# Delta-rule attention with a quantized FFN on one core: the first span rebuilt, with rounding constants made by ScalarE

## What is computed

```python
def l2n(x):
    return x / jnp.maximum(jnp.sqrt(jnp.sum(x * x, axis=-1, keepdims=True)), 1e-12)

def _quantized_matmul(x, w, scale):
    wq = w.astype(jnp.float8_e4m3fn).astype(x.dtype)
    y = jnp.einsum('bsi,io->bso', x, wq)
    return y * scale

def step(S, inp):                       # delta rule, over the 4096 tokens
    qt, kt, vt, bt = inp
    v_pred = jnp.einsum('bhk,bhkv->bhv', kt, S)
    delta = (vt - v_pred) * bt[..., None]
    S = S + kt[..., None] * delta[:, :, None, :]
    return (S, jnp.einsum('bhk,bhkv->bhv', qt, S))

xn = _layernorm(x, axis=-1)
q, k, v = l2n(heads(xn @ Wq)) * dh ** -0.5, l2n(heads(xn @ Wk)), heads(silu(xn @ Wv))
beta = jax.nn.sigmoid(xn @ Wb)
o = delta_rule(q, k, v, beta)           # scan of step
o = o * jax.lax.rsqrt(jnp.mean(o * o, axis=-1, keepdims=True) + EPS) * o_norm_weight
attn = o.reshape(b, l, d) @ Wo
gate = silu(_quantized_matmul(xn, gate_w, gate_scale))      # 512 x 1536
up = _quantized_matmul(xn, up_w, up_scale)                  # 512 x 1536
ffn = _quantized_matmul(gate * up, down_w, down_scale)      # 1536 x 512
return x + attn + ffn
```

## Time and profile before

| | us |
|---|---|
| median of 3 runs | 2445.73 |
| lowest and highest run | 2445.45, 2448.61 |
| the profiled execution, its own time | 2442.38 |
| its span, first to last instruction | 2440.6 |

### The profile page before, as it was taken

How to read it: one execution, slowest core, us unless ns; L and a number is a source line. 1 busy time by engine, 2 the same in 40 slices (tenths; PEclk the granted TensorE clock), 3 DMA queues, 4 the chain that set the end, 5 groups by cost and what they waited for, 6 DMA issues and landing times.

```text
span 2440.6 us, 90080 instructions
## 1 busy us (share of the span) xinstructions
PE 2314.6 (95%) x40944; PEld 1259.3 (52%) x40944; DVE 1817.7 (74%) x3210; ACT 861.2 (35%) x2069; POOL 275.0 (11%) x521
## 2 busy tenths in 40 slices
PE   1869999999999999999999999999999999999996
PEld 0435555554655545455554555555465554545553
DVE  7985866869677695867769586686967769586785
ACT  2353432524234252423425243242423425242341
POOL 3011002010010101001010110201001010100100
PEclk9989999999999999999999999999999999999999
DMA  6100100100010010100001010010101001010000
GB/s 216 48 1 4 36 3 3 36 3 36 4 36 3 3 36 3 36 3 12 27 3 36 3 36 3 3 36 3 36 4 36 3 3 36 3 36 3 11 28 19
DMA packets 27163, 54.30 MB, mean 22 GB/s; under 512 B 5152, under 2 KB 5152, under 8 KB 26784
## 3 DMA queue, kind: packets, MB, share of 16 engines
q1 hardware_dynamic: 26784, 48.55, 5.7%
HBM read 31.76 MB, written 16.78 MB: 20 GB/s over the span
## 4 chain that ended last, share of the span: by engine, by line
PE 93%; DVE 4%; issue 1%; SPq 1%; DMA 0%; POOL 0%; ACT 0%; POOLq 0%; DVEq 0%
PE T L350 22%; PE D L425 21%; PE D L502 15%; PE D L435 14%; PE D L436 13%; PE D L366 7%; PE D L355 1%; DMA ds_row<-in_L_ffn_down_scale_dram 0%; DVE wd L267 0%; DVE wgu L267 0%; DVE w_lo L921 0%; DVE outer_v L1145 0%; DVE at L1152 0%; SPq L300 0%; SPq L295 0%
## 5 line engine op out<-in xcount | busy, mean ns | idle before, releaser
L435 PE MATMUL D<-xt_hi,wgu 128*128 128x512 f16 x1536 | 586.3, 382 | 18.5 <-ACT sg L674 12.1
L436 PE MATMUL D<-xt_lo,wgu 128*128 128x512 f16 x1536 | 584.7, 381 | 0.0
L425 PE MATMUL D<-xt_hi,w_hi 128*128 128x512 f16 x832 | 317.1, 381 | 38.5 <-DVE wo_lo L925 38.5
L425 PE MATMUL D<-xt_lo,w_hi 128*128 128x512 f16 x832 | 316.5, 380 | 0.0
L502 PE MATMUL D<-wd,f_hi 128*128 128x512 bf16 x768 | 293.6, 382 | 0.3 <-issue 0.3
L425 PE MATMUL D<-xt_hi,w_lo 128*128 128x512 f16 x768 | 292.3, 381 | 0.0
L502 PE MATMUL D<-wd,f_lo 128*128 128x512 bf16 x768 | 291.1, 379 | 0.0
L1152 DVE TENSOR_TENSOR at<-at,outer_v 128x62 f32<-128x62 f32 (+15 forms) x496 | 262.4, 529 | 12.8
L1145 DVE TENSOR_TENSOR outer_v<-mt,at 128x62 f32<-128x62 f32 (+15 forms) x496 | 260.7, 526 | 11.7
L435 PEld LDWEIGHTS D<-xt_hi,wgu 128*128 128x128 f16 x1536 | 150.5, 98 | 195.7 <-ACT sg L674 12.6
L436 PEld LDWEIGHTS D<-xt_lo,wgu 128*128 128x128 f16 x1536 | 150.9, 98 | 167.4 <-issue 2.8
(11 more groups left out here) (169 smaller groups left out, 3207.4 us busy)
## 6 DMA issues: line engine op xcount, KB each, us to landing
xs<-_attn_hidden_states_dram SPq DMA_DIRECT2D x34, 512.0 KB, 3.4
out_dram<-xs SPq DMA_DIRECT2D x32, 512.0 KB, 3.1
f_hi<-in_L_ffn_down_w_dram SPq DMA_DIRECT2D x2, 768.0 KB, 6.8
f_lo<-in_L_ffn_down_w_dram SPq DMA_DIRECT2D x2, 768.0 KB, 8.3
qt<-in_L_ffn_gate_w_dram SPq DMA_DIRECT2D x2, 768.0 KB, 4.3
kpv<-in_L_ffn_up_w_dram SPq DMA_DIRECT2D x2, 768.0 KB, 4.3
qt<-in_L_attn_Wq_dram SPq DMA_DIRECT2D x1, 1024.0 KB, 10.2
kpv<-in_L_attn_Wk_dram SPq DMA_DIRECT2D x1, 1024.0 KB, 13.1
```

The source lines that it names most:

```text
L425: last = nc.tensor.matmul(D[bank][:, :], w[:, k, cols], xp[:, k, :], start=n == 0, stop=n == len(products) - 1)
L435: nc.tensor.matmul(D[bank][:, :], wgu[:, k, c:c + P], xt_hi[:, k, :], start=k == 0, stop=False)
L436: last = nc.tensor.matmul(D[bank][:, :], wgu[:, k, c:c + P], xt_lo[:, k, :], start=False, stop=k == KT_ - 1)
```

## The change

It touches only the first span and what comes before it.

- **Constants.** ScalarE makes abs(w) * 2^20 as bf16 in one activation (`magnitude_of`), into other places than before. VectorE then computes max(c, 1.5 * 2^14) - w and max(c, 1.5 * 2^14) - that, two SCALAR_TENSOR_TENSORs per piece, in place of four instructions. For the two GpSimd pieces VectorE applies the max (`unit_of`).
- **Loads.** Wk comes before Wq; pieces 2 to 5 get stages of their own and are issued early; Wb and the norm weight are issued by ScalarE; the three scale vectors are issued behind piece 6. The norm weight has its own semaphore, `onw_loaded`.
- **Weights.** The order of largest magnitudes, high and low parts and rounding is changed on VectorE; Wk comes first. TensorE waits at job 0 for the low part of Wk only, at the other jobs for Wq's, at V for all.
- **Norms.** The eight squares have eight buffers, and the 96 one-column products run in one go behind job 8, in bank 3. The root of the bound is taken by GpSimd ahead of the Newton steps for k.
- **VectorE's loop.** In the first span too, V's transposes stand in the solve loop; two down pieces stand at steps 14 and 18; the fuses have a table of their own, starting at step 22. Two memsets are moved to the front.
- **ScalarE.** The 12 scalings of `wd` stand in pairs behind the silus of tiles 4 to 9; in `order` rows below their line is L726.

```diff
-NORM_BANK = 0
+NORM_BANK = 3
+LEAST, STEP_UP = 1.5 * 2.0 ** 14, 2.0 ** 20
+FUSE_FIRST_AT = {22: 0, 26: 1, 30: 2, 34: 3, 38: 4, 43: 5, 48: 6, 53: 7, 59: 8}
+DOWN_PIECE_AT = {14: 2, 18: 3}
...
+            load_w(1, kt, wk)
             load_w(0, qt, wq)
-            load_w(1, kt, wk)
+            load_piece(P_PIECES)
             load_w(2, vt, wv)
-            sp.dma_start(wb_raw[:, :, :], wb.rearrange("(k p) c -> p k c", p=P)).then_inc(w_loaded[3], 16)
-            for h in range(QUADS):
-                sp.dma_start(onw4[32 * h:32 * h + 32, :], onw.rearrange("(d o) -> d o", o=1), allow_slow_non_contiguous=True).then_inc(small_loaded, 16)
             load_w(4, pt, wo)
-            load_piece(P_PIECES)
-            load_piece(P_PIECES + 1)
...
+            for n in range(P_PIECES + 1, P_PIECES + 4):
+                load_piece(n)
             for n in range(P_PIECES):
                 sp.wait_ge(p_rounded, n + 1)
                 load_piece(GU_PIECES + 2 * n)
                 load_piece(GU_PIECES + 2 * n + 1)
...
+            sp.wait_ge(v_rounded, 3)
+            load_piece(P_PIECES + 4)
+            sp.dma_start(gs[:, :], gate_s.rearrange("(c p) -> p c", p=P), allow_slow_non_contiguous=True).then_inc(small_loaded, 16)
...
+            sp.dma_start(ds_row[:, :], down_s.partition_broadcast(P)).then_inc(small_loaded, 16)
+            sp.wait_ge(v_rounded, 4)
+            load_piece(P_PIECES + 5)
...
-            pe.wait_ge(proj_ready, 5)
...
+                        if opening and job in JOB_V and bank_of(job) == NORM_BANK:
...
+                        if opening and not first:
+                            pe.wait_ge(proj_ready, 2 if job == JOB_K[0] else 5 if job in JOB_V else 3)
...
+                    if opening:
+                        pe.wait_ge(kwide_ready, MS)
+                        for n in range(GU_PIECES):
+                            pe.wait_ge(sq_ready, n + 1)
+                            for c in range(IC):
+                                last = nc.tensor.matmul(D[NORM_BANK][:, 12 * n + c:12 * n + c + 1], squares[n][:, c * P:(c + 1) * P], ones[:, :],
+                                                        start=True, stop=True)
+                            last.then_inc(norms_full, 1)
                     gram(4)
                     gram(5)
                     project(9, end=5)
...
+                nc.scalar.activation(magnitude(n), stage[where], ACT.Abs, scale=STEP_UP).then_inc(magnitude_ready, 1)
+            for n in range(P_PIECES):
+                magnitude_of(n)
...
-            act.wait_ge(small_loaded, 16 * 7)
+            magnitude_of(P_PIECES)
+            act.wait_ge(onw_loaded, 16 * QUADS)
...
+            for n in range(P_PIECES + 1, P_PIECES + 4):
...
+            for n, src in ((1, kt), (0, qt), (2, vt)):
...
+            magnitude_of(P_PIECES + 4)
+            def square_of(n):
+                if n < P_PIECES:
+                    act.wait_ge(p_rounded, n + 1)
+                    act.wait_ge(proj_ready, 3)
+                else:
+                    act.wait_ge(v_rounded, (n if n < 6 else 7) - P_PIECES + 1)
+                    act.wait_ge(proj_ready, 4 if n in (4, 5) else 3)
+                nc.scalar.activation(squares[n], rounded_home(n), ACT.Square).then_inc(sq_ready, 1)
...
+                    if opening:
+                        magnitude_of(GU_PIECES - 1)
...
+                    if opening:
+                        square_of(0)
+                        square_of(1)
+                        magnitude_of(GU_PIECES)
+                        magnitude_of(GU_PIECES + 1)
+                        beta_tanh()
+                        square_of(2)
+                        evacuate_k(2)
+                        square_of(3)
+                        square_of(4)
+                        evacuate_q(2)
+                        square_of(5)
+                        evacuate_k(3)
+                        square_of(6)
+                        square_of(7)
+                        evacuate_q(3)
+                        magnitude_of(GU_PIECES + 2)
+                        magnitude_of(GU_PIECES + 3)
+                        act.wait_ge(small_loaded, 48)
...
+                        if opening and ic >= 4:
+                            act.wait_ge(wd_rounded, PIECES - GU_PIECES)
+                            for row in (2 * ic - 8, 2 * ic - 7):
+                                ins = nc.scalar.activation(wd[:, row, :], wd[:, row, :], ACT.Identity, scale=row_inv[:, row:row + 1])
+                            if row == IC - 1:
+                                ins.then_inc(wd_ready, 1)
...
+                    if opening:
+                        pool.wait_ge(bound2_ready, 1)
+                        pool.nop(nofuse=True)
+                        nc.gpsimd.tensor_tensor(b_b[:, :], b_a[:, :], pos_half[:, :], ALU.pow).then_inc(bound_ready, 1)
...
+                w, c = stage[slot(n)[0]], magnitude(n)
+                dve.wait_ge(magnitude_ready, n + 1)
+                one(nc.vector.scalar_tensor_tensor(w, c, LEAST, w, ALU.max, ALU.subtract))
+                nc.vector.scalar_tensor_tensor(rounded_home(n), c, LEAST, w, ALU.max, ALU.subtract).then_inc(done, 1)
...
+            def unit_of(n):
+                dve.wait_ge(magnitude_ready, n + 1)
+                nc.vector.tensor_scalar(magnitude(n), magnitude(n), LEAST, None, ALU.max).then_inc(unit_ready, 1)
...
+            one(nc.vector.memset(state[:, :, :, :], 0.0))
+            nc.vector.memset(ssq[:, :], 1.0).then_inc(ffn_ready, 1)
+            unit_of(0)
             dve.wait_ge(rstd_ready, 1)
             for j in range(TILES):
                 layer_norm_apply(j, 0).then_inc(xn_ready, 1)
+            unit_of(1)
+            largest(1, flat(kt))
...
+            rounded(P_PIECES, v_rounded)
             dve.wait_ge(onw_done, 1)
             largest(4, flat(pt))
-            for n in range(P_PIECES, P_PIECES + 2):
-                rounded(n, v_rounded)
+            rounded(P_PIECES + 1, v_rounded)
+            rounded(P_PIECES + 2, v_rounded)
...
+            one(nc.vector.tensor_scalar(wb_out[:, :, :, 0:MS], wb_in, w_scale[:, 3:4], None, ALU.mult))
...
+            dve.wait_ge(hi_ready, 1)
+            low_w(1, kt)
+            dve.wait_ge(hi_ready, 2)
+            low_w(0, qt)
+            rounded(P_PIECES + 3, v_rounded)
+            dve.wait_ge(hi_ready, 3)
+            low_w(2, vt)
...
-                        for n in range(P_PIECES + 2, GU_PIECES):
-                            rounded(n, v_rounded)
-                            if n == P_PIECES + 3:
-                                b_to_tokens()
-                        dve.wait_ge(v_rounded, GU_PIECES - P_PIECES)
-                        one(nc.vector.memset(state[:, :, :, :], 0.0))
+                        rounded(GU_PIECES - 2, v_rounded)
+                        b_to_tokens()
+                        rounded(GU_PIECES - 1, v_rounded)
                         dve.wait_ge(consts, 3 + QUADS)
-                        nc.vector.memset(ssq[:, :], 1.0).then_inc(ffn_ready, 1)
...
                         for n in range(2):
                             rounded(GU_PIECES + n, wd_rounded)
-                            dve.wait_ge(wd_rounded, n + 1)
-                        for m in range(MS):
-                            v_to_tokens(m)
-                        for n in range(2, 4):
-                            rounded(GU_PIECES + n, wd_rounded)
-                            dve.wait_ge(wd_rounded, n + 1)
                         gate_up_bound()
                         set_diagonal(0)
...
+                    fuse_at = FUSE_FIRST_AT if opening else FUSE_AT
...
-                        if op in V_AT and not opening:
+                        if op in V_AT:
                             v_to_tokens(V_AT[op])
                         if opening and op == SCALE_AT:
                             gate_up_scale()
...
+                        if opening and op in DOWN_PIECE_AT:
+                            rounded(GU_PIECES + DOWN_PIECE_AT[op], wd_rounded)
+                        if op in fuse_at:
+                            fuse_tile(fuse_at[op])

```

152 lines of the change are left out of this document (52 added, 100 removed).

## The result

The changed kernel takes **2417.9 us** (median of 4 runs, 2415.18 to 2421.81) against 2445.59 for the kernel before (4 runs, 2441.31 to 2448.61). The ratio is 0.9892, 95% interval 0.9881 to 0.9904: 27.7 us less, where 29.7 were forecast. The profiled execution took 2418.15 us, with a span of 2416.3.

The account below looks back on a forecast made before the run. VectorE was taken to bound the first 234 us, behind TensorE's waits. The loop's end 28.5 us earlier plus 1.2 for the wd scaling made 29.7, so 2445.7 becomes 2416.0 us; range 2411 to 2424.

Parts of the forecast that it names:

- The price of a piece: VectorE's rounding: two instructions of 1.79 us replace four, saving 1.88 us on each of 10 pieces, 18.8 us.
- rival (b): VectorE's rounding: the mixed bf16/f32 form costs 2.22 us, 8.6 us over 20 instructions, giving 2424.6; chance 0.05.
- The start of the projections: Opening of the first span: job 0 waits only for Wk's low part and starts at 45.5 us instead of 58.25.
- rival (c): Opening: more is won, as POOL's 9.4 us follow the maxima and TensorE's clock holds; 2411 to 2413, chance 0.08.
- the onw wait of 6.7 is gone: Opening: VectorE's 6.7 us wait for the norm weight applied to Wo, traced to a DMA, disappears.
- From there to the solve loop: First span, from first projection to first solve step: the solve loop starts at 88.8 us instead of 122.78.
- rival (a): Before the solve loop: a helper, ScalarE or a load, binds and costs 4 to 8 us; 2420 to 2424, chance 0.14.
- late next: Before the solve loop: norms cost TensorE 3 us, covered by VectorE with 1.8 us to spare; first to slip.
- The loop: First span's solve loop grows from 50.99 to 56.4 us and ends at 145.2 instead of 173.77, 28.5 us earlier.
- Rival (d): Gate-up in the loop: TensorE's clock never rises between short waits, 30.3 us more, 2446.3; chance 0.02.
- The moved fuses cost nothing: Solve loop: VectorE sets the pace, so fuses starting at step 22 add no time.
- The 1.2 us for the scaling of wd: Behind the loop: scalings between silus remove most of a 1.5 us TensorE stand, winning 1.2 us.

Follow-up runs that it names:

- e1: Changed kernel with two more one-input passes over the elements in each of VectorE's ten roundings; 2435.32 us, ratio 0.9951.
- b1: Changed kernel with VectorE's first-span order changed: last maximum and scales earlier, pieces moved, three down pieces before the bound; 2422.35 us, ratio 0.9896.
- e7: Changed kernel with GpSimd's second pair of additions made to wait until VectorE has rounded piece 2; first projection at 49.3 us.
- e2: Changed kernel with the three scale vectors loaded right behind Wo and ScalarE's product of Wo waiting for them; 2420.6 us in one run.
- e4: Changed kernel with the first span's fuses at the steps of the other spans, the first at step 29; 2418.07 us in one run.
- e5: Changed kernel with ScalarE's 12 scalings of wd in one block, as before the change; 2419.57 us in one run.
- e10: Changed kernel with the 96 norm products cut into four blocks of 24, three products of job 9 between each two; 2423.58 us, ratio 0.9902.
- b3: Changed kernel with VectorE's order changed again, norm products in four blocks, and gate products ahead of the wait at the loop's end; 2419.34 us, ratio 0.9877.

## Why the prediction was right, step by step

**The price of a piece** was right: 1.79 forecast, 1.75 and 1.76 measured, for one bf16 and one f32 input, with f32, f16 or bf16 output; rival (b), 2.22, is out. The abs on ScalarE took 1.48 against 1.5. e1 shows that these instructions are indeed on the path that sets the end: given back, 19.9 us of them cost 14.2.

**The start of the projections** came out at 45.16 for 45.5 by luck: two errors cancel. GpSimd's result was forecast for 39.5 and was there at 34.2, earlier even than the 37.1 that rival (c) took, and not for the reason of (c), that the time follows the maxima (b1, below). VectorE was forecast to wait 1.6 us for it from 37.9 and instead was itself busy until 39.06, 2.2 of that for the port that GpSimd held. The forecast had left this collision out: it summed the additions and the pieces each for itself, although its own times let them overlap (additions until 28, piece 2 from 24.8). What sets the all-reduce's start is left open. In the changed kernel it came 6.12 us behind the last addition and just behind the last maximum (32.22). In b1, where the last maximum was there at 28.17, it still came 6.1 behind the addition, at 32.62:

```profile
32.62 0.40 POOL L793 PARTITION_ALL_REDUCE amax_all<-amax  x1 [6.12 <-issue]
```

In e7 it was 7.2 behind it, and in no kernel less than 6.0. A part of that time is therefore GpSimd's own; why it was 9.41 in the earlier trace rows no run here tells.

**The loads.** ScalarE issued wb_raw and onw in 0.48 and 2.20 us, where SP had taken 3.83 and 4.43; the table was loaded by 4.8 and the first abs stood at 9.11, waiting for its data. Timeline of the queues, and ScalarE's product, which waits for Wo alone:

```profile
0.81 0.48 ACTq L568 DMA_DIRECT2D wb_raw<-in_L_attn_Wb_dram  x1
...
1.32 2.20 ACTq L570 DMA_DIRECT2D onw<-_attn_o_norm_weight_dram  x4
```

```profile
23.98 2.00 ACT L592 ACTIVATE kpv<-kpv,onw 128x2048 f32<-128x2048 f32 x1 [1.26 <-DMA kpv<-in_L_attn_Wo_dram]
```

The step "the onw wait of 6.7 is gone" holds; e2 adds that the order alone would have hidden most of it.

**From there to the solve loop** 44.94 for 43.3. The bound was ready at 84.0 (84.9 forecast), K3's evacuation stood at 72.0 (73.1), piece 7's abs ended at 56.5 (58.0): ScalarE was earlier than feared, and rival (a), a helper that binds, did not come. VectorE's wait for K3's evacuation, 1.7 us where 0.9 was forecast, looks like the rival's sign, but ScalarE itself had waited for TensorE there (0.62). The start of TensorE was read wrongly: the forecast says 3.4 us at 1.2 GHz "as before", but before the change 14 products were slow, for 5.9 us. It did no harm, since the jobs' distances were taken from that same trace; that this time varies from 2.9 to 5.9 us in equal code, and moves the solve loop by up to 1.2, was not foreseen. What slipped is what the forecast named as "late next", the norms, but not by their length (2.5 us, forecast 3): behind them the clock fell to half, the grams took 2.62 (123 of 128) and 3.06 where they take 2.0 at full clock, and VectorE, which came to them 0.5 earlier than forecast, waited 1.51 us. In e4 and e5, where the low clock lasted half as long, it waited 0.21 and 0.36. Another 0.6 is the first transpose of V, which stands just ahead of the first solve step and was counted in the loop.

**The loop** took 54.90 for 56.4. That transpose is 0.6 of it, the two pieces took 6.9 instead of 7.2, and the last 0.6 are not accounted for. Of the old wait for the bound nothing is left.

**TensorE in the loop.** It waits for fuse, not for silu, from its restart at 112.29 (forecast 112.6). Rival (d), that the clock never rises in this rhythm, is out. Windows of that stretch (length, TensorE busy, granted clock, DMA share, GB/s):

```profile
112.30:116.00 3.70, 3.70 (x10) 0.56 0.29 113
116.00:120.00 4.00, 4.00 (x20) 1.00 0.02 4
...
132.00:136.00 4.00, 3.20 (x15) 1.00 0.00 0
136.00:140.00 4.00, 3.40 (x16) 1.00 0.00 0
```

Eight products at half clock, then 2.4 GHz for the rest. The gaps came out smaller than forecast at first, probably because the late start had let banks fill; from 128 us on there is one in each 4 us, of 0.36, 0.90 and 0.60, and the clock stays. The Trainium skill's rule (TensorE: Matmul & The Clock Gate, section "A second HAM failure mode: psum-queue depth-cycling"), that short idle times between groups of products can make the clock swing, did not come true at this length of gap; the clock did fall in the 3.88 us without work at the loop's end, and behind the unbroken block of one-column products. "The moved fuses cost nothing" is right, and e4 adds that they also bring nothing.

**Behind the loop** 60.99 for 59.4. The 1.2 us for the scaling of wd is the term that was wrong. The wait of 1.54 us before the change is gone, but TensorE now runs out of gate products 3.88 us before the transposed solution is there, and the clock reads 0.50 from 146.3 to 149.7, where it stayed at 1.00 behind the 1.57 us without work before. The one makes up for the other: the last gate product starts 19.3 us behind the loop's end before and 19.1 after, so 0.2 us are won, and e5, with the block put back, is at 19.3. The forecast had no term for that clock. The other part of the stretch took 41.9 us against 41.3, within the 40.9 to 42.2 of equal code. All this makes the gain of the first span 28.4 instead of 29.7, by +0.3 (start), -1.6, +1.5 and -1.6.

**The sum** was thus 2416.0 for a measured 2417.9, inside the range of 2411 to 2424. The last 0.7 us between the 28.4 of the marks and the 27.7 of the medians are within what the later spans vary.

## What to carry to other kernels

Price a faster instruction from the trace's row for the same memory and size, and then ask at what time it runs now: an instruction that moves forward may meet another engine's at a port that they share, and that cost stands in no row of the trace before. Where an engine is nearly full beside another, take work off it in the place where nothing else binds (here the opening and the loop gave the full price, the middle less than half of it). Look at what stands behind a block of very small matrix products: it may run at half clock, and in e10 and b3 some ordinary products strewn between kept it up. And before a gain of 1 or 2 us is read from one mark of one trace, compare places that the edit can't have touched: TensorE's slow start alone moved that mark by up to 1.2 us here.

## What the hardware showed that was not expected

- VectorE's instructions with two SBUF inputs, and a 0.96 us TENSOR_SCALAR, stand still for the rest of a GpSimd addition that began first (3.92, 2.74, 4.53 and 3.29 us), and GpSimd's for VectorE's (4.48 instead of 3.10). A TENSOR_REDUCE is not held. A MEMSET of GpSimd holds the TENSOR_SCALAR (2.56) and not the form with two inputs (1.76).
- Behind 96 matrix products of one column, 2.5 us, followed by small ones of 32 rows, TensorE's clock fell to 0.50 for 3.4 or 6.8 us; with three products of 512 columns between each 24 it stayed at 1.00. Gaps of 0.36 to 0.90 us between full products left it at 1.00.
- Behind the long wait at the start 7 to 14 products ran at the pitch of half clock, in equal code, and in after and before the granted clock of the profile reads 1.00 there; only the pitch of 0.43 shows it.
- The issue of one and the same small load took very different times: us 4.40 us before, 0.73 after and 6.48 in e2; onw 4.43 on SP's queue and 2.20 at the very start on ScalarE's. What it depends on no run separates.
- A span of unchanged code takes between 144.2 and 148.0 us from one to the next, so that the whole program's time repeats only within 8. The first span's marks repeated within 0.6 us in the two profiles of the changed kernel, and in equal code within some 2.
